# A hybrid layer on one core: silu of the expert tiles on ScalarE, four at a time, through both banks

## The reference

```python
x = x + _L0_attn_a_ref(_layernorm(x), ...)   # h = exp(delta*A)*h + delta*B*x, then sums over the states
x = x + _L0_ffn_ref(_layernorm(x), Wg, W1, W2, W3)
x = x + _L0_attn_b_ref(_layernorm(x), ...)   # diagonal recurrence
x = x + _L0_ffn_ref(_layernorm(x), Wg, W1, W2, W3)
```

```python
h = jnp.einsum('nc,ech->enh', xf, W1)
g = jnp.einsum('nc,ech->enh', xf, W2)
y = jnp.einsum('enh,ehc->enc', jax.nn.silu(h) * g, W3)
out = jnp.einsum('enc,ne->nc', y, combine)
```

## Time and profile before

| | |
|---|---|
| median of 3 runs | 1955.55 us |
| the profiled execution | 1953.74 us |
| its span | 1951.8 us |
| VectorE busy | 86% |
| GpSimd busy | 78% |
| TensorE (matmul) busy | 70% |
| ScalarE busy | 58% |
| last scan begins at | 1767.1 us |

### The profile page before, as it was taken

The page is one execution under the profiler, slowest core; times in us unless marked ns, Lnnn a source line. Parts: engine busy times, 40 slices in busy tenths (PEclk is TensorE's granted clock), DMA queues, the critical chain, the costliest instruction groups (busy, mean ns, idle before and its releaser), DMA issues. The chain is left out here.

```text
span 1951.8 us, 19610 instructions
## 1 busy us (share of the span) xinstructions
PE 1370.1 (70%) x5928; PEld 601.9 (31%) x5928; DVE 1677.1 (86%) x2365; ACT 1140.2 (58%) x2176; POOL 1518.8 (78%) x888
## 2 busy tenths in 40 slices
PE   3236458777777778778776778778686887568857
PEld 1001113234332433224331333224331343224424
DVE  3978989999898999999898999999898999995433
ACT  4547556665676566765576556666567566554313
POOL 0899889878897789888898788887897798974112
PEclk8556569889897999989897999979897889879979
DMA  3500400031001300031001400031000400000000
GB/s 101 194 0 25 183 0 1 25 111 68 11 1 64 139 11 1 25 108 70 12 1 45 157 12 1 25 108 71 11 1 27 175 6 1 1 6 1 6 1 6
DMA packets 34145, 88.38 MB, mean 45 GB/s; under 512 B 5364, under 2 KB 20599, under 8 KB 25847
## 3 DMA queue, kind: packets, MB, share of 16 engines
q1 hardware_dynamic: 32454, 87.12, 12.5%
q10 hardware_dynamic: 1584, 0.01, 0.0%
HBM read 75.58 MB, written 11.53 MB: 45 GB/s over the span
## 5 line engine op out<-in xcount | busy, mean ns | idle before, releaser
L848 POOL TENSOR_TENSOR w<-ur,br 128x1024 f32<-128x1024 f32 x512 | 1200.2, 2362 | 194.7 <-DVE h L1156 182.4
L1156 DVE TENSOR_TENSOR_SCAN h<-da,w 128x512 f32<-128x512 f32 x1024 | 1205.7, 1209 | 79.0 <-ACT da L739 33.4
L739 ACT ACTIVATE da<-dr,al 128x511 f32<-128x511 f32 x1024 | 689.9, 691 | 196.2 <-DVE h L1156 194.6
L568 PE MATMUL ys<-h,wsum 128*32 128x512 f32 x2048 | 325.8, 713 | 231.7 <-DVE h L1156 208.5
L687 ACT ACTIVATE tq<-bankH 128x512 f32<-128x512 f32 x256 | 152.8, 597 | 403.9 <-PE bankH L501 403.0
L501 PE MATMUL bankH<-nT,w 128*128 128x512 f32 x512 | 308.0, 686 | 95.0 <-DVE sq L1086 94.8
L501 PE MATMUL bankG<-nT,w 128*128 128x512 f32 x512 | 291.9, 653 | 56.7 <-DVE aq L1095 56.5
L792 POOL TENSOR_TENSOR x<-x,yk 128x512 f32<-128x512 f32 x128 | 163.1, 1274 | 169.0 <-ACT yk L700 168.4
L514 PEld LDWEIGHTS bankY<-w,aq 128*128 128x128 f32 x2048 | 261.3, 202 | 98.7 <-issue 72.4
L514 PE MATMUL bankY<-w,aq 128*128 128x128 f32 x2048 | 266.6, 286 | 16.9 <-DVE aq L1095 12.7
L1086 DVE SCALAR_TENSOR_TENSOR sq<-tq,bankH 128x512 f32<-128x512 f32 x256 | 171.1, 668 | 84.1 <-ACT tq L687 83.8
(11 more groups left out here) (172 smaller groups left out, 822.5 us busy)
## 6 DMA issues: line engine op xcount, KB each, us to landing
br<-b_rows SPq DMA_DIRECT2D x32, 1024.0 KB, 11.7
dr<-d_rows SPq DMA_DIRECT2D x16, 1024.0 KB, 7.6
ur<-u_rows SPq DMA_DIRECT2D x16, 1024.0 KB, 6.8
d_rows<-vh SPq DMA_DIRECT2D x16, 256.0 KB
u_rows<-th SPq DMA_DIRECT2D x16, 256.0 KB
xnew<-in_L_attn_a_x_dram SPq DMA_DIRECT2D x8, 256.0 KB, 3.1
w<-in_L_ffn_W_dram SPq DMA_DIRECT2D x2, 1024.0 KB, 14.6
x<-in_L_attn_a_x_dram SPq DMA_DIRECT2D x8, 256.0 KB, 7.6
```

The lines of the kernel that those rows point to most:

```text
L568: ins = nc.tensor.matmul(ys[32 * q:32 * q + 32, :], wsum[:, :], h[:, (2 * group + q // 2) % H_RING, q % 2, :], start=(n == 0), stop=(n == ...
L739: A(da[duo % D_RING][:, k % 2, 1:L], dr[:, half, q, 1:L], ACT.Exp, scale=nega[:, QUADS * half + q, n:n + 1]).then_inc(decay_ready, 1)
L848: G.tensor_tensor(w[:, duo % W_RING, :, :], ur[:, half, q:q + 2, :], br[:, n:n + 1, :].to_broadcast([128, 2, L]), ALU.mult).then_inc(produ ...
L1156: V.tensor_tensor_scan(h[:, duo % H_RING, k % 2, :], da[duo % D_RING][:, k % 2, :], w[:, duo % W_RING, k % 2, :], 0.0, ALU.mult, ALU.add). ...
```

## The change

- ScalarE writes silu(h) itself, from the bank into one of four buffers (`zt`, the two halves of `tq` and of `sq`); this frees the bank. VectorE's first product goes, and its second multiplies the silu by the W2 tile. W3 is multiplied by 0.5.
- The tiles come in blocks of four, every 11 slots. Tiles 0 and 2 of a block use bank H, tiles 1 and 3 bank G, first for the W1 tile and then for the W2 tile. TensorE has all four W1 tiles in the block's first slot, and the W2 tiles 2, 3, 7 and 8 slots later (`GATED_STEPS`).
- ScalarE has the four silus of a block in one slot, three after the W1 tiles (`SILU_LAG`); VectorE's products come two slots after the W2 tile (`AQ_LAG`); the outputs 9 and 13 slots after the block's start (`OUTPUT_STEPS`).
- The gap's tanh has a step of its own, in slot 35 of the turn for layer 1 as before (`GAP_STEP`).

```diff
-Y_LAG = 4
-ACT_LAG, TANH_LAG = 3, 2
+ACT_LAG, SILU_LAG, AQ_LAG = 3, 3, 2
+GATED_STEPS, OUTPUT_STEPS = (2, 3, 7, 8), (9, 13)
...
-def tile_at(j):
+def silu_at(m, j):
-    return QUARTER_SLOTS * j // 4
+    return MOE_AT[m] + QUARTER_SLOTS * (j // 4)
...
-        PE_STEPS.append((tile_slot(_m, _j), "late" if is_late_tile(_m, _j) else "post", "H", f"h{_m}_{_j}"))
-        PE_STEPS.append((tile_slot(_m, _j) + 1, "late" if is_late_tile(_m, _j) else "post", "G", f"g{_m}_{_j}"))
+        _kind, _bank = "late" if is_late_tile(_m, _j) else "post", "HG"[_j % 2]
+        PE_STEPS.append((tile_slot(_m, _j), _kind, _bank, f"h{_m}_{_j}"))
+        PE_STEPS.append((tile_slot(_m, _j, GATED_STEPS[_j % 4]), _kind, _bank, f"g{_m}_{_j}"))
...
-                        A(tq[:, j % 2, :], p[:, :], ACT.Tanh, scale=0.5).then_inc(hidden_tanh_ready, 1)
-                        if j == GAP_TILE:
-                            act.wait_ge(gap_ready, 2 * c + m)
-                            A(rc[:, 2, :], rc[:, 3, :], ACT.Tanh, scale=0.5).then_inc(gap_tanh_ready, 1)
+                        A(zt[j % 4], p[:, :], ACT.Silu).then_inc(drained[BANK[f"h{m}_{j}"]], 1)
+                    elif name == "gap":
+                        act.wait_ge(gap_ready, 2 * c + m)
+                        A(rc[:, 2, :], rc[:, 3, :], ACT.Tanh, scale=0.5).then_inc(gap_tanh_ready, 1)
...
-                    G.tensor_scalar(part, part, 0.25, None, ALU.mult).then_inc(outputs_scaled, 1)
+                    G.tensor_scalar(part, part, 0.5, None, ALU.mult).then_inc(outputs_scaled, 1)
...
-                    if name == "h":
-                        p = got(t, f"h{m}_{n}")
-                        v.wait_ge(hidden_tanh_ready, 4 * E * c + 2 * E * (m - 1) + n + 1)
-
-                        drain(f"h{m}_{n}", V.scalar_tensor_tensor(sq[:, n % 2, :], tq[:, n % 2, :], 1.0, p[:, :],
-                                                                  ALU.add, ALU.mult))
...
-                        drain(f"g{m}_{n}", V.tensor_tensor(aq[:, n % 4, :], sq[:, n % 2, :], p[:, :], ALU.mult))
+                    drain(f"g{m}_{n}", V.tensor_tensor(aq[:, n % 4, :], zt[n % 4], p[:, :], ALU.mult))
```

More of the change, by code:

```diff
@@ L51, in is_late_output, with tile_slot @@
     return m == 2 and e >= FIRST_LATE_OUTPUT
-def tile_slot(m, j):
-    at = MOE_AT[m] + tile_at(j)
+def tile_slot(m, j, step=0):
+    at = silu_at(m, j) + step
     return max(0, at - PAIRS) if is_late_tile(m, j) else at
 def output_slot(m, e):
-    return LATE_OUTPUTS[e] if is_late_output(m, e) else MOE_AT[m] + max(tile_at(2 * e + 1) + 1 + Y_LAG, 7 if e == 0 else 0)
+    return LATE_OUTPUTS[e] if is_late_output(m, e) else silu_at(m, 2 * e) + OUTPUT_STEPS[e % 2]
 S5_AT = output_slot(1, E - 1) + SUM_LAG - 3
@@ L75 @@
 FIRST_LOADS, PROJECTION_LOADS, LATE_LOADS, EXPERT_LOADS = 6, 13, 12, 3
-GAP_TILE = 2
+GAP_STEP = 7
 KINDS = ("late", "post", "pre")
@@ L125, in moe_v @@
 def moe_v(m, late):
-    return sorted([(SLOT[f"h{m}_{j}"] + 1, "h", j) for j in tiles_in(m, late)]
-                  + [(SLOT[f"g{m}_{j}"] + 1, "g", j) for j in tiles_in(m, late)], key=lambda s: s[0])
+    return [(SLOT[f"g{m}_{j}"] + AQ_LAG, j) for j in tiles_in(m, late)]
 def moe_act(m, late):
-    return sorted([(SLOT[f"h{m}_{j}"] + TANH_LAG, "h", j) for j in tiles_in(m, late)]
+    return sorted([(SLOT[f"h{m}_{j}"] + SILU_LAG, "h", j) for j in tiles_in(m, late)]
+                  + ([] if late else [(MOE_AT[m] + GAP_STEP, "gap", 0)])
                   + [(SLOT[f"y{m}_{e}"] + WEIGH_LAG + n, "y", 2 * e + n) for e in outputs_in(m, late) for n in range(2)],
@@ L259, in hybrid_kernel @@
         gap_ready = sem("gap_ready"); gap_tanh_ready = sem("gap_tanh_ready"); routed = sem("routed")
-        hidden_tanh_ready = sem("hidden_tanh_ready"); weighted = sem("weighted"); added = sem("added")
+        weighted = sem("weighted"); added = sem("added")
         sin_ready = sem("sin_ready"); turned_ready = sem("turned_ready"); diagonal_scanned = sem("diagonal_scanned"); real_ready = sem("real_ready")
@@ L1079, in moe_tiles @@
                 c = t.b - 2 if is_late else t.b - 1
-                for slot, name, n in moe_v(m, is_late):
+                for slot, n in moe_v(m, is_late):
                     yield slot
-                    if name == "h":
-                        p = got(t, f"h{m}_{n}")
-                        v.wait_ge(hidden_tanh_ready, 4 * E * c + 2 * E * (m - 1) + n + 1)
-                        drain(f"h{m}_{n}", V.scalar_tensor_tensor(sq[:, n % 2, :], tq[:, n % 2, :], 1.0, p[:, :],
-                                                                  ALU.add, ALU.mult))
[L1088 to L1094, removed]
-                        drain(f"g{m}_{n}", V.tensor_tensor(aq[:, n % 4, :], sq[:, n % 2, :], p[:, :], ALU.mult))
+                    p = got(t, f"g{m}_{n}")
+                    v.wait_ge(drained[BANK[f"h{m}_{n}"]], t.before(f"h{m}_{n}") + 1)
+                    if is_late and not is_late_output(m, n // 2 - 2):
+                        v.wait_ge(filled["Y"], t.begin("Y"))
+                    elif n >= 4:
+                        v.wait_ge(filled["Y"], t.before(f"y{m}_{n // 2 - 2}") + 1)
+                    drain(f"g{m}_{n}", V.tensor_tensor(aq[:, n % 4, :], zt[n % 4], p[:, :], ALU.mult))
             def post(t):
```

## The result

The changed kernel takes **1938.6 us** (1938.3 to 1940.3, four runs) against 1954.8 of the kernel before on the same chip: a ratio of 0.992, 95% interval 0.990 to 0.993. It is faster by 16 us where 81 were forecast. Its span is 1936.6 us at a mean granted TensorE clock of 0.843; the profiled execution of the kernel before has 0.857.

The account below looks back on a forecast made before the run. VectorE, busy 86% of the span, was taken as the bound, with GpSimd close behind. 1953.74 less 59 us in the scanning and 22 after the last scan is 1872.7; 1.8 for the median gives 1874.5 us, range 1825 to 1940.

Parts of the forecast that it names:

- the forecast's chain: In a block, from the bank coming free to the next exponential: 7.4 us against VectorE's 6.2, so a 1.2 us wait.
- the sum of the stalls: VectorE's waits in A and C, about 1.2 us per ordinary block, taken off what the deleted products save.
- A and C: Stretches of a steady turn bound by VectorE: second expert layer up to its last late tile (77.33 us); first expert layer (73.70).
- VectorE gives up 18.6 us per turn: In a full scanning turn: 32 deleted products at 0.58 us each, half in each of A and C.
- A switch is 1.36 us, and nothing beside its load: On ScalarE: each added table switch costs the load of 1.28 us and 0.08 of lost overlap, with no drain.
- Late block: Second layer's block at slot 10, with four normalizations before ScalarE returns: a chain of 8.9 us against 5.1, stall 3.8.
- First blocks of the layers, and slot 0: Blocks starting with empty banks: stall equals the old wait for the first tanh, 1.09 us; slot 0 hides its stall.
- B and D stay: The short gap (13.69 us) and the diagonal layer with the next batch's projections (57.12) keep their times.
- After the last scan: In the final 184 us TensorE runs without holes: 10 saved twice and 2 for late tiles, 22 us, bounds 14 and 26.
- The floor: Rival for the scanning: stalls hide and GpSimd sets the time; about 1820 us in all, chance 0.1.
- TensorE late: Rival for the blocks: W1 tile 0 starts 2 us late, sums behind it too; 10 us a turn, about 1932, chance 0.15.
- A switch at twice its load: Rival on ScalarE: each switch takes 2.7 us instead of 1.36; about 1988 us in all, chance 0.09.

Follow-up runs that it names:

- lead3: The changed kernel with ScalarE waiting for one scan more before each decay, so three scans ahead of VectorE, not four: 2034.0 us, ratio 1.040.
- gates32: The changed kernel with the scan layer's gates and residual scaling twelve slots earlier: 1928.3 us, ratio 0.985.
- relief: The kernel before with VectorE's first product left out and bank H freed by the tanh, no blocks or added loads: 1872.05 us, ratio 0.958.
- tanh_block: The changed kernel with tanh(h/2) for the silu, so blocks stay and the 109 added table loads go: 1895.3 us, ratio 0.970.
- znorm: The changed kernel with the four normalizations of z one slot later, behind the late block: 1939.3 us, ratio 0.991.
- pairs_gates: The changed kernel with blocks of two silus, and the scan layer's gates and residual scaling twelve slots earlier: 1883.5 us, ratio 0.964.
- ring3: The changed kernel with a third double buffer of decays, placed in SBUF, so ScalarE may be six scans ahead: 2162.3 us, ratio 1.106.

## Why the prediction was wrong

Two steps failed. **The first** is "The exponentials run at most six scans ahead of VectorE (three buffers of two)". There are two double buffers of decays, and the limit is in the code (here of after):

```python
D_RING, W_RING, H_RING = 2, 3, 4
act.wait_ge(scanned, PAIRS * t.b + k - 2 * D_RING + 1)
```

Two of two, a lead of four; three is GpSimd's ring. (The words on the kernel ahead of the prediction, "three double buffers" and "six tiles ahead", have the same mistake.) With six, by the forecast's chain, the decay ahead of a block is written early, the load is over when tile 0 fills, and the chain is 7.4 us. With four that decay waits for scan s-1, which ends 1.1 us after the chain has begun (958.99); load, silu and tile 2 follow, and the chain is 8.4. The stall is 2.3 us instead of 1.2. Four products are worth 2.3, so such a block earns nothing. lead3 shows that the lead acts on the price. That six scans in PSUM would have given the forecast is argued, not shown.

**The second** is the sum of the stalls, in which VectorE waits for decays, and for GpSimd 0.9 us in C ("so I take 4.8"), and for nothing else. In A and C it holds 9.1 us for decays, with layer 1's first block 10.2; the runs have 14.5. Of the 4.3 more, the first step gives 1.1 at slot 43 and 0.6 at slot 120; the rest stands elsewhere (below). State sums had no term and take 4.9; GpSimd has 3.7 instead of 0.9; a W2 tile takes 1.2. Two of a turn's block stalls stand behind such waits, those of slots 54 and 65: in gates32, where GpSimd's wait at slot 52 is gone, 2.29 us for a decay appear at slot 54:

```profile
972.91 1.22 DVE L1146 TENSOR_TENSOR_SCAN h<-da,w 128x512 f32<-128x512 f32 x1 [2.29 <-ACT da L736]
```

So 59 us of scanning gain came to 0.3 by several waits, and the lead's own share is not separated: relief, tanh_block and the changed kernel give 23 us to the blocks and 43 to the loads in them, but a longer lead was not tested.

Step by step:

- *VectorE gives up 18.6 us per turn*: right as work (205.5 to 186.4 in the turn). *Worth of it*: relief's turn of 211.4 to 213.6 is about the 213 of the forecast, but by another sum. With no blocks at all the saved work of 18.5 us yields only 8 to 10, and the forecast, which took off 10.1 for stalls and GpSimd, got the same by chance. GpSimd's floor in C was seen (4.8 taken, 4.5 found).
- *The silu's price*: 0.597 taken, 0.597 found. *A switch is 1.36 us, and nothing beside its load*: right; the silu starts 0.02 us after the load's end (961.00 after 959.70 + 1.28).
- *Late block*: 3.8 forecast, 5.28 found, since ScalarE stood waiting for an output ahead of it. The normalizations in it were costed at 1.5, and znorm takes 1.5 of it away.
- *First blocks of the layers, and slot 0*: 1.1 forecast for layer 1's, 2.08 found, with its W1 tiles at the lower clock (0.54). The block at slot 0 was to cost nothing, and costs 1.11 and 1.23 us.
- *B and D stay*: nearly for D (58.40 after, 59.08 before); B is 3.1 us shorter, with the wait for the layer's first tanh and one of 1.27 for decays gone. A and C give just that back: the steady turn is 221.86, and was 221.84.
- *Not in the sum*: VectorE's wait for state sums (`ys`), 11.0 to 39.7 us in all. The sum at 1000.99 is held by three W1 tiles of 2 us, the first of which waited 3.17 us for a product of VectorE's, late itself behind two waits for GpSimd; the tiles ahead of the sum that ends at 856.4 wait for nothing of VectorE's.
- *After the last scan*: 22 forecast, 14.9 found, within its bounds of 14 to 26. TensorE does run without holes (10.99 of 10.99, clock 1.00), and the term that was mis-sized is the matmul: 0.87 was taken from one row; in a row the pitch is 0.85 to 1.02, four tiles and two outputs take 11.0 us, not 10.5, and 1.4 are saved per four tiles instead of 1.9. Ten such groups make 14. The second layer takes 47.1 us (1884.16 to 1931.26) where 44 were forecast.

The rivals. *The floor*: false for the change, and the bound of C in relief and pairs_gates. *TensorE late*: its 1932 us lie near, its mechanism by half. In an ordinary block W1 tile 0 starts when VectorE frees the bank (1.61 us of idle before it), so TensorE has time, though less than the rival's sum had: its two matmuls, output and sums are 4.7 us by the earlier trace rows (0.96, 0.86, 1.88, 1.0), not 4.0. The sums behind the W1 tiles are late, as that rival said. *A switch at twice its load*: false, by those 0.02 us; of the drain that the Trainium skill ("ScalarE: Activation LUTs", What ACT_TABLE_LOAD costs) adds, they show nothing, here as in the kernel before.

The signs that the prediction named did speak: the wait for decays rose to 127.5 us, above the 70 to 100 named, and a steady turn of 221.9 instead of 213 told at once that the gain was gone in the scanning.

## What to carry to other kernels

When work that can't be interrupted (a block with its table loads) is put into an in-order engine that feeds another, hold its length against the lead that the ring allows, and read the ring's depth from the constant and the wait in the code, not from a picture of it. Here the stand was longer than the lead and an ordinary block gave its saving back; two short stands with twice the switches beat one long one, with TensorE's tiles split as well. Then price every other supply of the engine that feeds on it, and not only the one that the change touches: the sums and GpSimd's products took more of the saving than the decays did beyond their forecast. Price a saving on the busiest engine by the next engine's share of that stretch, and rearrange that engine's work once the saving is there: the same edit was worth 3, 10 and 30 us.

## What the runs showed of the hardware

A scan whose two inputs both lie in SBUF and a product of GpSimd's slow each other down. In ring3 one scan in three reads its decays from SBUF. VectorE's timeline there:

```profile
958.07 3.29 DVE L1147 TENSOR_TENSOR_SCAN h<-da,w 128x512 f32<-128x512 f32 x1
...
965.19 1.22 DVE L1147 TENSOR_TENSOR_SCAN h<-da,w 128x512 f32<-128x512 f32 x1
```

and GpSimd's:

```profile
957.94 5.58 POOL L846 TENSOR_TENSOR w<-ur,br 128x1024 f32<-128x1024 f32 x2
...
964.68 2.36 POOL L846 TENSOR_TENSOR w<-ur,br 128x1024 f32<-128x1024 f32 x1 [1.17 <-DVE h L1147]
```

The scan at 958.07 has its decays in SBUF and takes 3.29 us beside two products, which are slower as well (2.79 us each); the one at 965.19 has them in PSUM and takes the usual 1.22 beside a product of the usual 2.36. The Trainium skill ("SBUF — State Buffer", Who interferes with whom) states that a VectorE instruction with two SBUF inputs contends with a GpSimd instruction that reads SBUF; the run agrees, and here it costs 1.0 us per such scan in the mean (three times 1551 - 1208 ns). Decays in PSUM are not only a place to put them: they keep the scan out of GpSimd's way.
